# A transformer layer on one core: the cross-attention chain and the third norm's second rows are moved forward in every settled slot

## The reference

```python
y  = layernorm(x)                                     # norm 0
y  = layernorm(y + attention(y, y, y, causal)) * g1 + beta1        # norm 1
ca = softmax(y @ ctx.T / sqrt(256)) @ ctx             # 64 context rows per sequence
y  = layernorm(y + ca) * g2 + beta2                   # norm 2
h  = relu(y @ w1 + b1)                                # 256 -> 1024   ("ff1")
y  = layernorm(y + h @ w2 + b2) * g3 + beta3          # 1024 -> 256  ("ff2"), norm 3
x1 = x + y
xq = fp4(layernorm(x1))                               # norm 4
h  = silu(xq @ fp4(w_gate).T) * (xq @ fp4(w_up).T)    # 256 -> 704, twice ("gate_up")
x2 = x1 + fp4(h) @ fp4(w_down).T                      # 704 -> 256  ("down")
```

## Time and profile before

| | |
|---|---|
| median of 3 runs | 600.66 us (599.99 to 603.07) |
| the profiled execution: device time, span | 600.61 us, 598.5 us |
| PE busy | 563.8 us, 94% of the span |
| PEld, DVE, POOL, ACT busy | 89%, 83%, 64%, 63% |
| granted clock of PE, mean | 0.989 |
| DMA engines | mean 32 GB/s, nothing waits for them after the start |

### The profile page before, as it was taken

One profiled execution on the slowest core, in us unless ns is written; L12 is line 12 of the kernel. 1 busy time (PEld: TensorE's weight loads), 2 busy tenths in 40 slices (PEclk: granted clock), 3 DMA queues, 4 the chain that ended last, 5 costly groups with the idle time before them and its releaser, 6 DMA issues.

```text
span 598.5 us, 12474 instructions
## 1 busy us (share of the span) xinstructions
PE 563.8 (94%) x4054; PEld 535.5 (89%) x4054; DVE 495.5 (83%) x1220; ACT 374.6 (63%) x779; POOL 385.8 (64%) x466
## 2 busy tenths in 40 slices
PE   4798879999999999999999999999999999999886
PEld 2677779999999999999999999999999999999785
DVE  4889898887988888887988888887988878877775
ACT  3666575766667575766667674866667674757231
POOL 3657667676767667675767666666767666675543
PEclk9797999999999999999999999999999999999999
DMA  7701010010201010010101010010201010000000
GB/s 228 241 2 37 0 28 19 1 55 1 62 1 55 2 34 30 0 53 0 61 0 53 0 42 19 0 53 0 61 2 35 3 36 1 19 2 19 0 10 27
DMA packets 18743, 19.31 MB, mean 32 GB/s; under 512 B 1536, under 2 KB 18192, under 8 KB 18704
## 3 DMA queue, kind: packets, MB, share of 16 engines
q1 hardware_dynamic: 18704, 18.82, 10.4%
HBM read 14.62 MB, written 4.19 MB: 31 GB/s over the span
## 4 chain that ended last, share of the span: by engine, by line
PE 73%; DVE 6%; POOL 5%; issue 5%; ACT 2%; POOLq 0%; DVEq 0%; ACTq 0%
PE R L1124 6%; PE R L1126 6%; PE R L1125 6%; PE O L1176 5%; PE TR L1029 5%; PE O L1239 4%; PE R L1194 4%; PE R L1196 4%; PE R L1195 4%; PE O L1241 4%; PE O L1240 4%; PE O L1218 3%; PE O L1220 3%; PE O L1219 3%; PE R L1029 3%
## 5 line engine op out<-in xcount | busy, mean ns | idle before, releaser
L461 POOL TENSOR_TENSOR rs<-mv,neg_half 128x1 f32<-128x1 f32 (+1 forms) x112 | 68.2, 619 | 32.1 <-DVE mv L1589 30.9
L1124 PE MATMUL R<-gu_hi,xqT_hi 128*128 128x352 f32 x240 | 80.2, 334 | 2.9 <-ACT hT L743 2.0
L1194 PE MATMUL R<-y2T_hi,w_hi 128*128 128x256 f32 x256 | 77.5, 303 | 4.6 <-ACT e_diag L777 1.7
L754 ACT ACTIVATE hqT_hi<-R 128x768 fp32r<-128x768 f32 x29 | 23.6, 812 | 86.8 <-PE R L1029 86.8
L1126 PE MATMUL R<-gu_hi,xqT_lo 128*128 128x352 f32 x240 | 77.3, 322 | 0.0
L1125 PE MATMUL R<-gu_lo,xqT_hi 128*128 128x352 f32 x240 | 77.2, 322 | 0.0
L1239 PE MATMUL O<-w_hi,hT_hi 128*128 128x256 f32 x256 | 74.5, 291 | 0.9 <-POOL hT_lo L496 0.9
L1196 PE MATMUL R<-y2T_hi,w_lo 128*128 128x256 f32 x256 | 73.2, 286 | 0.0
L1195 PE MATMUL R<-y2T_lo,w_hi 128*128 128x256 f32 x256 | 73.1, 285 | 0.0
L1241 PE MATMUL O<-w_hi,hT_lo 128*128 128x256 f32 x256 | 71.9, 281 | 0.0
L1240 PE MATMUL O<-w_lo,hT_hi 128*128 128x256 f32 x256 | 71.7, 280 | 0.0
(11 more groups left out here) (197 smaller groups left out, 1830.7 us busy)
## 6 DMA issues: line engine op xcount, KB each, us to landing
x_in<-in_x SPq DMA_DIRECT2D x16, 256.0 KB, 2.9
x_res<-in_x SPq DMA_DIRECT2D x16, 256.0 KB, 2.8
out<-x SPq DMA_DIRECT2D x32, 128.0 KB, 1.9
ctx_rows<-in_ctx SPq DMA_DIRECT2D x16, 64.0 KB, 2.5
hT<-in_L_xattn_w SPq DMA_DIRECT2D x1, 1024.0 KB, 7.3
hh<-in_L_xattn_w SPq DMA_DIRECT2D x1, 768.0 KB, 8.7
wd_raw<-in_L_ffn_w_down SPq DMA_DIRECT2D x1, 704.0 KB, 9.4
w_raw<-in_L_ffn_w_gate SPq DMA_DIRECT2D x1, 640.0 KB, 4.4
```

What stands on the lines that cost most here:

```text
L1124: mm(o, xh, gu_hi[:, c, m, cols], start=(c == 0), stop=False)
L1194: mm(o, w1_hi[:, c, cols], y2T_hi[:, c, :], start=(c == 0), stop=False)
```

## The change

Nothing is computed otherwise, and no instruction is added or taken away in a settled slot; only the lists of calls are written in another order, on PE, DVE, ACT and POOL. SP's list is unchanged. The head and the tail are unchanged, and slot 17 has the new order too.

- PE: `turn_z1` moves from between the third and fourth gate_up piece to just behind the scores; `cross` from behind gate_up to between two ff1 pieces, next to `turn_xq(0)`; `turn_cross` from the middle of ff2's first half to next to `turn_xq(1)`; `cross_values` from behind ff2's first half to before the fourth gate_up piece. ff2's first half is now one call over all eight blocks, and its second half follows it directly. `turn_hq(0)` comes after four blocks of the second half and not after two (FF2_TURN). `turn_y0` stands next to `turn_hq(1)`.
- DVE: norm 1's statistics, `cross_max`, `cp_lower`, `cross_sum` and norm 2's statistics come earlier; `ff_sum(b, h, 0)` now stands behind `h_scale` and `h_reciprocal` of t = 1; the statistics of norm 3's second rows open the slot.
- ACT: norm 1, `affine_turned`, `exp_cross` and `cp_upper` move ahead of `warm(Silu)`, which moves behind `exp_cross`; of relu's last two pairs the one stays before it and the other (3) comes after it; norm 2 comes before `hT_upper(0)`.
- POOL: `power` of norms 1, 2 and 3 and the gain rows of norm 1 move forward; scale_h(0), h_lower_last stand in the same order as before.

The diff, cut to its core:

```diff
         FF2_CUT = 5 * FC // 8
-        FF2_TURN = FC // 4
+        FF2_TURN = FC // 2
...  POOL, slot
                 if f1:
                     gamma3(b, g, 0)
                     x1_sum(b, g, 0)
+                    power(3, b, g, F, (1,))
                 if q1:
                     unscale_h(b, g, 1)
...
                 if q:
                     scale_h(b, h, 0)
                 if f:
                     h_lower_last(b, h)
-                if a:
-                    y_rows(b, h, True, 0)
-                    y_rows(b, h, True, 1)
                 if live(b, h + 1, 0):
                     power(0, b, h + 1, 0, (0, 1))
+                if a:
+                    power(2, b, h, A, (0, 1))
                 if q:
                     unscale_h(b, h, 0)
...  ACT, slot
+                if a:
+                    norm(1, b, h, A, 0, 1, z1[:, 0, :], z1[:, 0, :])
+                    norm(1, b, h, A, 1, 1, z1[:, 1, :], z1[:, 1, :])
...
+                if f:
+                    relu(b, h, (2,))
+                if q:
+                    xT_upper(b, h, 0)
+                if a:
+                    exp_cross(b, h)
+                if q:
+                    warm(b, h, ACT.Silu, 0)
+                if f:
+                    relu(b, h, (3,))
...  PE, slot
                 if q:
                     ready_for_gate_up(b, h)
                     gate_up(b, h, 0, 0)
                     turn_xq(b, h, 1)
+                if a:
+                    turn_cross(b, h)
+                if q:
                     gate_up(b, h, 0, 1)
                     gate_up(b, h, 1, 0)
                 if a:
-                    turn_z1(b, h)
+                    cross_values(b, h)
                 if q:
                     gate_up(b, h, 1, 1)
-                if a:
-                    cross(b, h)
                 if f:
                     ready_for_ff2(b, h)
-                    ff2(b, h, 0, range(FF2_CUT))
-                if a:
-                    turn_cross(b, h)
-                if f:
-                    ff2(b, h, 0, range(FF2_CUT, FC))
-                if a:
-                    cross_values(b, h)
-                if f:
+                    ff2(b, h, 0, range(FC))
                     ff2(b, h, 1, range(FF2_TURN))
...  DVE, slot
+                if f1:
+                    z3_stats(b, g, 1)
+                    aggregate(3, b, g, F, 1)
                 if a:
-                    self_reciprocal(b, h, 0)
-                    self_sum(b, h, 0)
+                    self_part(b, h, 0)
                 if q1:
                     h_lift(b, g, 1)
                     h_drop(b, g, 1)
...
+                if a:
+                    cross_sum(b, h)
+                    cross_stats(b, h)
                 if q:
                     h_product(b, h, 1, 1)
-                if a:
-                    cross_max(b, h)
-                if q:
                     h_lift(b, h, 0)
                     h_drop(b, h, 0)
                     h_max(b, h, 1)
...
                 if a:
-                    cp_lower(b, h)
-                    cross_reciprocal(b, h)
-                if f:
-                    ff_sum(b, h, 0)
+                    shift(2, b, h, A, (0, 1))
                 if q:
                     h_scale(b, h, 1)
                     h_reciprocal(b, h, 1)
...
+                if f:
+                    ff_sum(b, h, 0)
                     z3_stats(b, h, 0)
                     aggregate(3, b, h, F, 0)
```

More of the change, by code:

```diff
@@ L515, in slot @@
                 f1, q1 = live(b, h, Q), live(b, h, Q + 1)
+                front = live(b, h, 0)
                 g = h - 1
@@ L828, in slot @@
                     norm_x(b, h)
+                if f1:
+                    norm(3, b, g, F, 1, T, z3[:, 1, :], z3[:, 1, :])
                 if q1:
                     hT_upper(b, g, 1)
-                if isinstance(b, int) and HALVES * b + h == Q:
+                if early:
                     w_upper(act, 4)
@@ L838, in slot @@
                 if f1:
-                    norm(3, b, g, F, 1, T, z3[:, 1, :], z3[:, 1, :])
                     abs_x(b, g, 0)
-                if f:
-                    if not early:
-                        relu(b, h, (0, 1))
-                    relu_upper(b, h, (0,))
+                if f and not early:
+                    relu(b, h, (0, 1))
                 if front:
@@ L847, in slot @@
                     exp_rest(b, h)
+                if a:
+                    affine_turned(b, h, A, n1_turned, y1T, g1_col, beta1_col, y1T_set)
                 if f:
-                    relu_upper(b, h, (1,))
-                if q:
-                    if isinstance(b, int) and HALVES * b + h == Q:
-                        w_upper(act, 5)
-                    warm(b, h, ACT.Silu, 0)
-                    xT_upper(b, h, 0)
+                    relu_upper(b, h, (0,))
                 if f1:
@@ L882, in slot @@
                 if a:
-                    exp_cross(b, h)
-                    cp_upper(b, h)
+                    norm(2, b, h, A, 0, 1, z2[:, 0, :], z2[:, 0, :])
+                    norm(2, b, h, A, 1, 1, z2[:, 1, :], z2[:, 1, :])
                 if q:
@@ L1321, in slot @@
                 if f:
-                    ff1(b, h, (2, 3))
+                    ff1(b, h, (1, 2, 3))
                 if front:
@@ L1326, in slot @@
                     scores_rest(b, h, range(T))
+                if a:
+                    turn_z1(b, h)
                 if isinstance(b, int) and HALVES * b + h == Q:
@@ L1332, in slot @@
                     ff1(b, h, (4, 5))
+                if a:
+                    cross(b, h)
                 if q:
@@ L1801, in slot @@
                 if f1:
-                    x_norm(b, g, 1)
-                    x_max(b, g, 1)
-                    x_scale(b, g, 1)
-                    x_reciprocal(b, g, 1)
+                    x_lift(b, g, 1)
+                    x_drop(b, g, 1)
+                if isinstance(b, int) and HALVES * b + h == Q:
+                    w_lower(5)
+                if a:
+                    cross_max(b, h)
+                if q:
+                    xT_lower(b, h, 0)
                 if f:
                     h_lower(b, h, (1,))
-                if isinstance(b, int) and HALVES * b + h == Q:
-                    w_lower(5)
-                if q:
-                    xT_lower(b, h, 0)
                 if q1:
                     down_add(b, g, 1)
-                if f1:
-                    x_lift(b, g, 1)
-                    x_drop(b, g, 1)
-                if a:
-                    wait(dve, z1_set, b, h, A, T, T)
-                    stats(1, b, h, A, 0, z1)
-                    stats(1, b, h, A, 1, z1)
-                    aggregate(1, b, h, A, 0)
-                    aggregate(1, b, h, A, 1)
+                if h == 1 and live(b, h, 1):
+                    ctx_lower(b)
                 if front:
@@ L1828, in slot @@
                 if a:
-                    shift(1, b, h, A, (0, 1))
+                    cp_lower(b, h)
+                    cross_reciprocal(b, h)
                 if f:
```

90 lines of the change are left out of this document (37 added, 53 removed).

## The result

| | us |
|---|---|
| before, median of 6 runs | 601.35 (599.99 to 604.26) |
| changed, median of 6 runs | 651.18 (650.52 to 653.74) |
| ratio | 1.0823 (1.0796 to 1.085) |
| predicted | 628.0 (613 to 641) |
| span of the profiled execution, before and changed | 598.5, 649.7 |

Slower, as forecast, but by 50 us and not 27. First the page's busy shares and the same two slots by stretch, answering to the earlier trace rows (columns as there). By the count of the slots (n = 2b + h) these two are 9 (h = 1) and 10 (h = 0), not 10 and 11 as the rows and the prediction call them; nothing in the sums hangs on it.

What follows compares the result with a forecast made beforehand. PE sets the pace with almost no idle time, so each new wait lengthens a slot. 600.6 plus 18.9 (term A), 1.2 (slot 17) and 7.0 (terms B and C) gave 627.7, so 628 us; range 613 to 641.

Steps and rivals of the forecast that it cites:

- term A: Around ff2's first half: each slot 1.35 us longer (bounds 1.0 and 1.8), 18.9 us over 14 slots.
- step 3: DVE, with cross_sum and norm 2's statistics ahead, starts ff_sum 4.3 us after gate_up's fourth piece; PE continues at 4.75.
- step 1: ff2's first half waits for POOL's h_lower_last and starts 1.05 us after gate_up's fourth piece.
- What there is to gain: The wait before cross_values goes, at most 3 to 4 us over 14 slots; turns side by side save 0.
- Step 2: ff2's second half waits until ff_sum has read the bank: 0.87 us from the first half's last matmul.
- Term B: relu's end delays gate_up (0, 1) with h=0 by 0.3 us; two other h=0 edges add 0.1 us each.
- Term C: Start of a slot, h=1: ff1 waits for DVE's y2T_lower, +0.5 us, bounds 0 and 0.8.
- Slot 17 and the tail: The same two waits at ff2 in slot 17: +1.2 us, and the tail hangs on it.
- the one that had ACT and DVE set the pace: The relu_upper-to-relu chain between ACT and DVE is late by 1 to 2 us every slot: 649 us, chance 0.10.

Runs made afterwards that it cites:

- ff2_fed_first: Changed kernel with one-input shifts, plus h_lower_last before scale_h(0), ff_sum(0) between lift and drop, ff2's second half before the turn: 634.5 us, ratio 1.055.
- ln3_put_back: Changed kernel with the second rows' third norm put back on all engines to its place in the kernel before: 656.1 us, ratio 1.090.
- ff2_split: Changed kernel with ff2's first half in two calls, six blocks then two: 661.1 us, ratio 1.099.
- sum_behind_max_split: Changed kernel with one-input shifts, ff_sum of the first rows right behind the second rows' maximum, and ff2's first half in two pieces: 619.4 us, ratio 1.031.

## Why the prediction was right in kind and wrong in size

In short: the two waits of term A were the right ones, but step 3 (when DVE comes to ff_sum) and, with h=0, step 1 were too short, as DVE's two-input instructions were taken at their free durations; and the wait of the scores for hT_lower(1) was put at nothing. Together these are 10 + 10 us of the 23 that the forecast is short.

- *PE sets the pace, and each wait on it lengthens the slot*: right. But for stretches of 3.4 us at half clock in slots 3 and 16, the settled slots lose their time with PE idle at full clock.
- *What there is to gain* (0.2 us before cross_values, 0 for turns side by side): that wait is gone, as said; it is inside the slots' sums.
- *Term A, steps 1 to 3*: the right waits at the right place, mis-sized. Second half at G + 5.81 (h=0) and G + 5.23 (h=1) for G + 4.75, so 2.4 and 1.8 us a slot for 1.35, 29 us in all for 18.9. Step 1 was 0.5 us short with h=0: I let DVE come to scale_h's input as before, but h_lower(2) in front of it took 1.19 us for 0.68 while POOL ran context_values. Step 2's hand-over, forecast at 0.87 us, was sound: 0.80 in ff2_fed_first, where DVE is not late, and here 356.28 - 355.87 = 0.41 of it, from ff_sum's start to PE. Step 3 was 1.1 us short in that slot (ff_sum at G + 5.40, not 4.3): 0.62 of it is norm 2's shift, taken at its free price, 0.44 that DVE reached the last h_product at G + 1.19 and not 0.75, the late h_lower(2) again. Rows 10 had shown that DVE's two-input instructions swing by more than a factor of two; I priced x_lift by it and not the shifts, as these are tiny. The size of the instruction did not matter: it ended when POOL's did.
- *Term B* (0.3 and 0.2): nothing. In the h=0 slot gate_up's pieces follow each other without a gap, though relu's last pair ends at 343.19 + 0.82 = 344.01 and gate_up (0, 1) starts at 344.15. It was as near as I said, on the other side.
- *Term C* (0.5 at ff1, h=1): not at ff1. ff1 starts 0.1 us after y2T_lower, at 291.23 against 291.13, so the room was used up, but PE came as late, as the down product in front of it had waited for z1's first sum: it starts 1.66 us after the turn of z2 (288.86 - 287.20), and 1.17 us in the kernel before. The statistics in front of z1's sum cost there, 0.5 us in an h=1 slot, what I had put at ff1. The size was right, the place was not.
- *Missing*: the scores, waiting for hT_lower(1), in 12 slots, up to 0.94 us. I had looked only at y2T_lower among the instructions at DVE's start of the slot that PE is close behind. After term A 3.03 - 2.4 = 0.6 us of a slot are left with h=0 and 3.62 - 1.8 = 1.8 with h=1: 17 us, for 7 forecast in B and C. By the distances from start to start, beyond the usual ones, 10 us of it are in front of the scores, 2.7 in front of the turn of z1 in slot 16, 2.4 in front of the down product in six h=1 slots; half clock behind the turn of z1 costs some 1.7 (an estimate, half of 3.4).
- *Slot 17 and the tail*: 4.1 us for 1.2. ff2 is 1.3 us longer there, as forecast. The rest are waits ahead of it that the forecast had at nothing: ff1 for y2T_lower 1.2 us, a down product 0.5, and gate_up for xqT_hi 1.5, where the kernel before has 0.6. By the start of ff2's second half all 4.1 us are lost.
- *The rivals*: 651 lies at the one that had ACT and DVE set the pace (649, chance 0.10), but not for its reason, so that is chance. No chain of ScalarE holds gate_up in these slots; what PE waits for is DVE's queue, with POOL's hold on it, and POOL's h_lower_last.

The sum, by the slots: 29 at ff2, 17 at the scores, the down product and the turn of z1, 4 from slot 17 on, 50 for the span's 51.2. By the runs, as steps from one kernel to the other: third norm first 7.5; z1's norm and the cross scores early 11.0 (to 619.7, shifts in one-input form); turn and values of the cross-attention moved, and what goes with them, 17.3; shifts with two inputs 14.2. The first has the two-input shifts too, and the steps depend on their order, as ln3_put_back shows.

What held the shifts is shown as far as the ends that fall together and the run without the second input go: 29 shifts of two inputs ended with a POOL instruction, mean 0.87 us for 0.14; 42 of the one-input form ran beside one in 0.20. The Trainium skill has the rule, "SBUF — State Buffer", section "Who interferes with whom": a VectorE instruction with two SBUF inputs contends with a GpSimd instruction that reads SBUF, for a port pair that the two share and that one locks against the other. The traces agree. For VectorE's modes that use both of its ports the same section of the Trainium skill says that whoever issues first has the shared pair for its whole instruction. That would explain h_div, an immediate-scalar instruction with one SBUF input; no run tests it. Open: whether some order keeps both z1's early norm and the slot's start; none of those tried did.

## What to carry to other kernels

Before a VectorE instruction with two inputs is moved, look at what POOL runs at its new place, and in the old trace for tiny instructions whose maximum is far above their median: a shift of one element took the rest of the POOL instruction beside it, up to 1.05 us of 1.39. Work that stands between a matmul group and the reader of its bank is cover, and queues of other engines are tuned to it, so move the cover only with the queues. Two waits in a row hide each other: undo both at once, or neither shows its price. And a held instruction that is made immune hands the hold to the next one in its queue.

## What the runs showed of the hardware

- An fp32 scalar_tensor_tensor of 128x1 with both inputs in SBUF took up to 1.05 us beside POOL's 1.39 us tensor_tensor; as tensor_scalar with a pointer operand 0.20 us. A 128x44 tensor_scalar with two immediates, 0.18 us alone, took 0.56 in the same place.
- PE to VectorE and back through one PSUM bank: 0.80 us from the start of the last matmul to the start of the next group, with a tensor_tensor of 128x256 (0.42 us) between, in 14 slots of 14 (ff2_fed_first).
- PE idle for 2.6 to 2.8 us at once, between full stretches, was followed by 3.4 us at 1.2 GHz in six slots of six in ff2_split; of its eight idle times of 1.9 to 2.1 us at this place one was, and those of up to 1.5 us at this place in sum_behind_max_split never.
